# Last stage of a token tower: the query and key parts reach their stack by twelve direct copies instead of a trip through device memory

## The reference, cut to what matters

```python
sx = jnp.einsum('bsh,ndh->bnsd', x, hl_w) + hl_b[None, :, None, :]
q = jnp.einsum('bnsd,neod->bneso', sx, wq)
k = jnp.einsum('bnsd,nod->bnso', sx, wk)
v = jnp.einsum('bnsd,nod->bnso', sx, wv)
scores = jnp.einsum('bnesd,bntd->bnest', q, k) * d ** 0.5 + causal
att = jax.nn.softmax(scores, axis=-1)
qkv = jnp.einsum('bnest,bntd->bnesd', att, v)
```

## Time and profile before

| | |
|---|---|
| runs, us | 3371.49, 3397.48 (median), 3411.12 |
| profiled execution, us | 3390.36, its span 3388.6 |
| last stage, first to last round start on PE, us from the span's start | 2033.5 to 3260.1, 32 rounds |
| PE busy | 3081.6 us, 91% of the span |
| DVE, ACT, POOL busy | 77%, 54%, 38% |
| granted TensorE clock, mean | 0.92 |
| DMA issues of the change | 192 for Q (187.5 KB), 192 for K (46.9 KB), 32 stores (843.8 KB) |

### The profile page before, as it was taken

The page is one execution under the profiler, slowest core; times in us unless marked ns, Lnnn a source line. Parts: engine busy times, 40 slices in busy tenths (PEclk is TensorE's granted clock), DMA queues, the critical chain, the costliest instruction groups (busy, mean ns, idle before and its releaser), DMA issues.

```text
span 3388.6 us, 81043 instructions
## 1 busy us (share of the span) xinstructions
PE 3081.6 (91%) x24964; PEld 2193.7 (65%) x24964; DVE 2615.6 (77%) x7699; ACT 1817.5 (54%) x4484; POOL 1301.8 (38%) x1368
## 2 busy tenths in 40 slices
PE   0699999999999899998999998999999999999995
PEld 0588888888888634444777776666666666666663
DVE  4788888888888578886888865788777777778773
ACT  0355555555555445554766643555555555555552
POOL 1443444434344144441000022445445444444432
PEclk9999999999999989997888867999889989989996
DMA  4100000000000000000000013443333333333420
GB/s 140 35 22 22 14 21 14 21 20 15 21 14 8 1 1 0 0 0 1 1 0 0 0 28 58 71 66 64 59 59 59 58 59 60 70 57 63 68 36 4
DMA packets 74280, 110.98 MB, mean 33 GB/s; under 512 B 20105, under 2 KB 65481, under 8 KB 73577
## 3 DMA queue, kind: packets, MB, share of 16 engines
q1 hardware_dynamic: 72936, 106.85, 16.9%
q10 hardware_dynamic: 1024, 0.39, 0.0%
HBM read 76.01 MB, written 30.82 MB: 32 GB/s over the span
## 4 chain that ended last, share of the span: by engine, by line
PE 25%; issue 9%; POOL 6%; DMA 6%; DVE 5%; SPq 2%; ACT 1%; POOLq 0%; DVEq 0%; ACTq 0%
DMA qe_K<-query_key_parts 4%; PE psum L2329 3%; PE psum L1660 3%; PE psum L2315 2%; PE psum L2343 2%; POOL qe_root L3032 2%; PE psum L2302 2%; DMA query_key_parts<-qe_parts 2%; PE psum L2366 2%; PE psum L1689 2%; PE psum L1677 1%; SPq L2221 1%; PE psum L1731 1%; SPq L2223 1%; POOL qe_parts L3014 1%
## 5 line engine op out<-in xcount | busy, mean ns | idle before, releaser
L2782 DVE TENSOR_REDUCE qe_top<-psum 125x1 f32<-125x375 f32 (+2 forms) x896 | 500.8, 596 | 238.1 <-PE psum L2302 235.7
L2589 ACT ACTIVATE qe_E<-psum 125x375 f32<-125x375 f32 (+1 forms) x896 | 459.0, 531 | 285.1 <-PE psum L2302 261.0
L2302 PE MATMUL psum<-bconst 125*125 125x125 bf16 (+2 forms) x1792 | 491.3, 274 | 0.0
L625 PE MATMUL psum<-Q,K 96*125 96x125 f32 (+3 forms) x2304 | 404.5, 311 | 0.5 <-ACT E L836 0.4
L2315 PE MATMUL psum<-qe_K,qe_Q 96*125 96x375 bf16 (+2 forms) x1536 | 332.0, 300 | 59.4 <-DMA qe_K<-query_key_parts 32.3
L625 PEld LDWEIGHTS psum<-Q,K 96*125 96x125 f32 (+1 forms) x2304 | 334.3, 189 | 24.5 <-issue 1.2
L2329 PE MATMUL psum<-qe_Q,qe_K 97*125 97x375 bf16 (+2 forms) x1536 | 336.8, 299 | 2.4 <-ACT qe_E L2589 2.0
L1175 POOL TENSOR_TENSOR Q<-rot 64x375 f32<-64x375 f32 (+1 forms) x256 | 305.7, 1213 | 73.4 <-DVE rot L976 61.4
L836 ACT ACTIVATE E<-psum 125x500 f32<-125x500 f32 x384 | 226.2, 589 | 172.7 <-PE psum L645 169.5
L2315 PEld LDWEIGHTS psum<-qe_K,qe_Q 96*125 96x125 bf16 x1536 | 182.4, 148 | 167.1 <-DVE qe_top L2782 71.6
L2302 PEld LDWEIGHTS psum<-bconst 125*125 125x125 bf16 x1792 | 266.4, 149 | 9.8 <-issue 6.9
(11 more groups left out here) (341 smaller groups left out, 7199.7 us busy)
## 6 DMA issues: line engine op xcount, KB each, us to landing
qe_Q<-query_key_parts SPq DMA_DIRECT2D x192, 187.5 KB, 6.2
query_key_parts<-qe_parts SPq DMA_DIRECT2D x32, 843.8 KB, 3.6
s_row<-scores SPq DMA_DIRECT2D x32, 366.2 KB
qe_K<-query_key_parts SPq DMA_DIRECT2D x192, 46.9 KB, 6.6
x_tokens<-x SPq DMA_DIRECT2D x32, 187.5 KB
x_chunks<-x SPq DMA_DIRECT2D x4, 750.0 KB
E<-x SPq DMA_DIRECT2D x4, 750.0 KB
out<-qe_hout SPq DMA_DIRECT2D x32, 93.8 KB
```

The costliest lines, as they stand in the source:

```text
L625: nc.tensor.matmul(out[:, first * TP:(first + n) * TP].rearrange("p (o q) -> p o q", o=n), t.K[0:rows(h), par, h, jt * TP:(jt + 1) * TP], ...
L2302: return nc.tensor.matmul(out, B("ident_b")[0:TP, 0:TP], rhs, start=False, stop=True, skip_group_check=True)
L2589: nc.scalar.activation(E[:, e % 2, a:a + width], bank[0:TP, 4 + n % 2, 0:width], ACT.Exp).then_inc(e_done, 1)
L2782: nc.vector.tensor_reduce(dst, src, AX, ALU.max).then_inc(m_read, 1)
```

## The change

The store to device memory, the wait for it and the memory tensor are gone. Each of the twelve copies now reads `parts` in place and writes `Q` or `K`, both on chip. For that the weights are laid out so that row d*8+n*2+a of a projected query block holds dimension d of head n, and row d*4+n of the key block likewise: 16 rows of `Q` or `K` are then the 128 (or 64) rows of `parts` in their order.

The six copies that read part 0 go when ACT has written the three pieces of part 0 (and `e_ready` allows), the other six when POOL has finished. ACT's `first_part(b, 0)` now waits for all twelve copies of sequence b-1 (`stacked`).

```diff
-    heads = z(D, 4, HE, 2, DH2)
+    queries, keys, values = z(D, 2, DH2, HE, 2), z(D, 1, 2, DH2, HE), z(D, 1, HE, 2, DH2)
...
-            heads[rows, e % 2, n, e // 2] = l["wq"][n, e].T
-        heads[rows, 2, n, 0] = l["wk"][n].T
-        heads[rows, 3, n, 0] = l["wv"][n].T
+            queries[rows, e % 2, :, n, e // 2] = l["wq"][n, e].T
+        keys[rows, 0, 0, :, n] = l["wk"][n].T
+        values[rows, 0, n, 0] = l["wv"][n].T
...
-                sp.wait_ge(parts_done, (b + 1) * NP)
-                sp.dma_start(qk_dram, parts[:]).then_inc(parts_stored, 16)
-                sp.wait_ge(parts_stored, (b + 1) * 16)
-                for g, (qp, kp) in enumerate(zip(q_parts, k_parts)):
-                    rows = slice(g * DH2, (g + 1) * DH2)
-                    sp.dma_start(Q[rows, slot].rearrange("d (a i) s -> d a i s", i=2), rows_of[qp, :, :, 0:2]
-                                 ).then_inc(stacked, 16)
-                    sp.dma_start(K[rows, slot], keys_of[0, kp, 2]).then_inc(stacked, 16)
+                sp.wait_ge(hi_done, (b + 1) * NP)
+                for first in (True, False):
+                    for g, (qp, kp) in enumerate(zip(q_parts, k_parts)):
+                        rows = slice(g * DH2, (g + 1) * DH2)
+                        if (qp == 0) == first:
+                            sp.dma_start(Q[rows, slot].rearrange("d q s -> d (q s)"), parts[:, qp, 0:2, :]).then_inc(stacked, 16)
+                        if (kp == 0) == first:
+                            sp.dma_start(K[rows, slot].rearrange("d h s -> d (h s)"),
+                                         parts[0:DH2 * HE, kp, 2, :]).then_inc(stacked, 16)
+                    if first:
+                        sp.wait_ge(parts_done, (b + 1) * NP)
...
                 if i == 0:
-                    wait(act, parts_stored, b * 16)
+                    wait(act, stacked, b * 32 * len(q_parts))
```

More of the change, by code:

```diff
@@ L215, in weight_layout @@
         for e in range(EE):
-            heads[rows, e % 2, n, e // 2] = l["wq"][n, e].T
-        heads[rows, 2, n, 0] = l["wk"][n].T
-        heads[rows, 3, n, 0] = l["wv"][n].T
-    k.add("w_heads", heads.reshape(D, 4, 128))
+            queries[rows, e % 2, :, n, e // 2] = l["wq"][n, e].T
+        keys[rows, 0, 0, :, n] = l["wk"][n].T
+        values[rows, 0, n, 0] = l["wv"][n].T
+    k.add("w_heads", np.concatenate([v.reshape(D, -1, 128) for v in (queries, keys, values)], 1))
     gw = z(128, EE, HE * EE)
@@ L2113, in slices, with query_experts @@
         return tensor, scalar, vector, gpsimd
-def query_experts(k, ctx, qk_dram, out):
+def query_experts(k, ctx, out):
     nc, nb, F, B, W, bank = k.nc, k.nb, k.F, k.B, k.W, k.bank
@@ L2178, in query_experts @@
         folded, set_up, p_ready, v_ready, nz_ready, nz_done, v_kept = map(sem, ("folded", "set_up", "p", "v", "nz", "nz_done", "v_kept"))
-        hi_done, full_done, parts_done, parts_stored, stacked = map(sem, ("hi", "full", "parts", "parts_stored", "stacked"))
+        hi_done, full_done, parts_done, stacked = map(sem, ("hi", "full", "parts", "stacked"))
         m_ready, m_read, neg_ready, neg_turned, maxT_kept = map(sem, ("m", "m_read", "neg", "neg_turned", "maxT"))
@@ L2208, in sync @@
         def sync(sp):
-            rows_of = qk_dram.rearrange("(a d) p i s -> p d a i s", d=DH2)
-            keys_of = qk_dram.rearrange("(h a d) p i s -> a p i d h s", a=2, d=DH2)
             def stack(b, slot):
@@ L3080, in one, with tower @@
     return h[:, bass.ds(b, 1), :].rearrange("p o f -> p (o f)")
-def tower(nc, nb, x, fpack, bpack, wpack, packs, s_dram, qk_dram, out):
+def tower(nc, nb, x, fpack, bpack, wpack, packs, s_dram, out):
     with ExitStack() as ctx:
@@ L3093, in tower @@
         with nc.cleanup_on_exit(), ExitStack() as c:
-            query_experts(k, c, qk_dram, out)
+            query_experts(k, c, out)
 def kernel(**inputs):
@@ L3111 @@
     out = nc.dram_tensor("out", (nb, S, D), F32, kind="ExternalOutput").ap()
-    qk_dram = nc.dram_tensor("query_key_parts", (128, 3, 3, S), BF16).ap()
     s_dram = nc.dram_tensor("scores", (nb * CI, TP), F32).ap()
-    tower(nc, nb, *args, (f, b, w), s_dram, qk_dram, out)
+    tower(nc, nb, *args, (f, b, w), s_dram, out)
     r = run_bass_kernel_spmd(nc, [arrays], core_ids=[0])
```

## The result

The change made the kernel 0.6% slower, which is clear of the noise but too small to count: 3403.54 us (median of 20 runs, 3392.34 to 3432.11) against 3385.13 us for the kernel before (20 runs). The ratio is 1.0062, with a 95% interval of 1.0038 to 1.0085. I had forecast 3485 us, slower. The profiled execution took 3429.28 us with a span of 3427.5 us. A round of sequence b starts on PE with the first L2315 of b, and rounds are numbered by b from 0.

What follows compares the result with a forecast made beforehand. PE was taken as the bound, with its stops at round starts and the clock falls behind them. 3390 + 97 us for 28 rounds - 6 gave 3481, about 3485 us against the runs, slower; range 3340 to 3520 us.

Steps and rivals of the forecast that it cites:

- What the clock makes of it: PE's mid-round stop of 1.8 us brings one fall of the clock per round, at 4.7 us each.
- Stops for the stack vanish: PE's waits at a round's first score matmul for the stack's loads, 32.3 us in 20 rounds, go away.
- The second six land 8.2 us after the parts: The six late copies, issued when the parts are done, complete the stack 8.2 us later instead of 18.0.
- Rival C: The second six take 6.2 us or less, so PE waits for neither: 3307 us, chance 0.16.
- ACT waits 3.8 us, PE stops 1.8 us: Each round first_part waits 3.8 us for all twelve copies, stopping PE 1.8 us before its second projection.
- An undisturbed round of 37.0 us: Delays of 2.3 us less what is given back, net 1.1 us, make an undisturbed round 37.0 us.
- give-back: PE regains 0.76 us of idle time before L2374 and 0.42 us at the next round's start.
- Three rounds of before, 122.65 us: The baseline read from the earlier trace: three last-stage rounds, 2489.24 to 2611.89, 40.9 us each.
- The sum: Three rounds take 133.0 us, +10.35; 28 rounds +97 us, less 6: 3481 us, about 3485 against the runs.
- the few us that I took off for the start: Some 6 us of stops for the stack go in the four rounds at the start and end.
- Rival A: PE's stop in mid-round does not lower the clock: 3349 us, faster by 1.2%, chance 0.17.
- rival D: The clock falls in one round of three only, the stop being near the threshold: 3393 us, chance 0.15.

Runs made afterwards that it cites:

- e3_memory_early: The kernel before, still through device memory, but part 0 is stored and its six copies loaded early, the rest later: 3321.89 us, ratio 0.9812 to the kernel before.
- e5_late_stack: The change with split semaphores, plus five serial copies that PE's first score matmul of each round waits for: 3480.39 us, ratio 1.0262 to the kernel before.
- d_more_serial: The change plus one 46.9 KB copy issued when the twelve have landed, with first_part waiting for it too: 3489.32 us, ratio 1.0316 to the kernel before.
- p_rate: The change with 192 KB copies within SBUF added behind its last store, into 16 or 128 rows; six into 16 rows went at 98 GB/s.
- e1_split_wait: The change with separate semaphores: first_part waits only for the early six copies, POOL for the late six: 3322.06 us, ratio 0.9821 to the kernel before.
- e2_none_early: The change with all twelve copies issued behind POOL's last part, none early: 3599.42 us, ratio 1.0633 to the kernel before.

## Why the prediction was wrong

**The step that failed is "What the clock makes of it":** "1.8 us is on the falling side", and one fall for each round "at the lower price of 4.7 us". That price was taken from falls at round starts, where the trace of before had all of them. In mid-round 6 stops of 21 had no fall and the others had 3.4 or 6.8 us of low clock, where the price stood for 10.2. What one cost: three steady rounds took 125.1 us; 3 x 37.6 of undisturbed rounds, 3.6 of the loop's stop and 4.5 for the fall behind it (e3_memory_early: 115.5 less 3 x 35.9 less 3.3) leave 4.2, that is 1.4 us for each mid-round stop instead of 4.7. Three of these make 9.9 us of the 133.0 that I had forecast. The forecast for three rounds missed by only 7.9, since two other terms were too low: the undisturbed rounds (37.0 instead of 37.6) hid 1.8 us of it and the loop's stop another 0.4. The fault was a price carried from one place to another; that the place matters is shown by e5_late_stack and d_more_serial. What about the place decides it was not tried, nor what chooses between 0, 3.4 and 6.8 us in mid-round.

Point by point:

- *Stops for the stack vanish:* right. None of the 20 is left.
- *The second six land 8.2 us after the parts:* 8.5, from the written side's rate, as argued; p_rate shows that side as the limit. Rival C, with its rate of 436 GB/s from the Trainium skill, "SBUF — State Buffer", Summary: rules for kernel authors, is excluded by the 98 GB/s of p_rate. That C decides at 6.2 us after the parts was right to 0.2.
- *ACT waits 3.8 us, PE stops 1.8 us:* 4.1 and 2.14, both longer by the 0.3 us of the copies.
- *An undisturbed round of 37.0 us:* 37.5 to 37.8. The net cost was 1.7 us instead of 1.1. 0.3 of it is the longer stop. The rest is a give-back that was reckoned too high: PE still idles 0.27 us before L2374, and the 0.42 us at the next round's start is partly taken back at L2354, where PE now waits for DVE. Before, then the change:

```profile
2292.70 0.33 PE L2354 MATMUL psum<-bconst,qe_neg 125*16 125x125 bf16 x3
```

```profile
2692.22 0.33 PE L2354 MATMUL psum<-bconst,qe_neg 125*16 125x125 bf16 x3 [0.27 <-DVE qe_neg L2787]
```

In e1_split_wait and e3_memory_early this wait is 0.57 us, and their undisturbed rounds take 36.0 and 35.9 us, as before's 35.9 with its stop for the stack: the 0.4 us that rival C counted on (rounds of 35.5) are not to be had.

- *Three rounds of before, 122.65 us:* the seven steady turns had 122.45, so this was sound.
- *The sum:* 125.1 and 124.3 us in two profiles of the change, against 122.5 before, are +1.9 to +2.7 for three rounds. Times 9.33 that is +17 to +25 us, and the medians lie 18 us apart. The forecast had +97. Counted out, the first nine rounds gave +9.4 us in both profiles (342.6 against 333.2) and the 21 steady ones +18.5 and +13.2; the few us that I took off for the start did not come. (Also, 3481 plus the 7 us between profile and median is 3488, not 3485.)
- *Rival A* (no fall, 3349) and *rival D* (one fall in three rounds, 3393): neither is what happened. D's time is within 11 us by luck: one full mid-round fall of 4.7 us in three rounds stands in it where 15 short ones in 21 rounds came to 4.2 us for three. The Trainium skill's rule behind A, "TensorE: Matmul & The Clock Gate", HAM oscillation, was too mild at round starts, where 1.14 us was followed by a fall, and says nothing of short falls like those in mid-round.

This also says where the gain of 1.8% went. Before had 14 falls in its 21 steady rounds, all at round starts, seven behind the loop's stops and seven behind stops for the stack. The change removes the latter (e3 shows what that is worth) and puts 15 short falls and 21 stops of 2.1 us into mid-round. Low clock in three rounds: 23.9 before, 22.8 after, 13.4 without either kind.

## What to carry to other kernels

When a buffer's readers change from one quick store to many slow copies, look for whoever waits to overwrite it, and give each part of the buffer a semaphore of its own, so that the next writer waits only for the part that it overwrites. Price a stop of TensorE by stops at the same place of the order, with the same work behind it: here 2.1 us in mid-round cost 1.4 us more through the clock, while a stop half as long at a round's start was followed by 10.2 us at the lower one. And try the early start by itself: e3_memory_early got all of the gain with a handful of changed lines.

## What the runs showed of the hardware

- A stop's place counts for the clock beside its length. At round starts stops of 1.1 to 3.9 us had 10.2 or 13.7 us of low clock, at least 10.2 of it behind the stop (e5_late_stack, 21 of 21); in mid-round stops of 1.9 to 2.3 us had 0, 3.4 or 6.8 (the change), and of 7.7 us 10.2 in 19 rounds and 6.8 in two, of which 3.5 to 6.8 us lay behind the stop (e2_none_early). Shorter stops at a round's start are not decided: before, one of 1.05 us and one of 0.71 us had none and one of 0.74 us had 10.2. What in the work behind the stop makes the difference was not tried; the score groups of a round's start are small matmuls, one after the other.
- A fall needs no long stop. In e1_split_wait three of the steady rounds (10, 19 and 28, each the one after a loop's jump) had 10.2 us of low clock from 1.5 to 1.8 us after their start, with no idle time ahead of their first matmul, and 0.57 us before a later one, which the undisturbed rounds have too. At 4.5 to 4.7 us a fall they are most of what e1 lacks against e3 in the table. This cause stays open. Round 10:

```profile
2376.47 0.32 PE L2318 MATMUL psum<-qe_K,qe_Q 96*125 96x375 bf16 x1
...
2377.63 0.33 PE L2357 MATMUL psum<-bconst,qe_neg 125*16 125x125 bf16 x3 [0.57 <-DVE qe_neg L2791]
```

```profile
2378.00:2388.20 10.20, 10.20 (x50) 6.46 (x51) 5.22 (x12) 3.91 (x8) 2.43 (x4) 0.50 0.06 15
```

- Copies within SBUF into 16 rows at a time cost 1.6 us for each further 192 KB (p_rate), and six of them went at 98 GB/s from first issue to last landing; into 128 rows six took 5.5 us, at SP's own pace of issue.
- PE stops for 3.0 to 4.1 us at the start of rounds 9, 12 and so on to 27, seven times, with a fall behind each, in every kernel here (in e5_late_stack its added wait stands in the same place). By the kernel's text these are the seven jumps of PE's three-round loop back to its start, so I take the jump for the cause, untested. Some 7.8 us for three rounds are left in the best versions where it stands (115.5 less 3 x 35.9).
